# 64 of 512 plain columns move to the other column groups in a graph layer's edge sum

## The reference

```python
s_j = silu(x_j[:, 384:] @ W1 + b1) @ W3 + b3        # x_j = x[src]
edge_basis = rbf * cutoff @ W2 + b2                 # 20 sines of the edge weight
s1, s2, s3 = thirds of (s_j * edge_basis)
v_msg = v_j * s1[:, :, None] + s3[:, :, None] * edge_attr1[:, None, :]
x = x + segment_sum(concat([v_msg, s2]), dst)
... second message: node-wise, h from norms, summed over the same edges
x = layernorm(input + x)
```

## Time and profile before

| | |
|---|---|
| time, median of 3 runs | 641.67 us (639.85 to 643.99) |
| profiled execution, span first to last instruction | 638.7 us |
| edge loop with gathers | about 50 to 535 us |
| PE busy, matmul records | 538.3 us (84%), 5281 |
| granted TensorE clock, mean | 0.936 |
| DMA, mean | 197 GB/s |

### The profile page before, as it was taken

How to read it: one execution, slowest core, us unless ns; L and a number is a source line. 1 busy time by engine, 2 the same in 40 slices (tenths; PEclk the granted TensorE clock), 3 DMA queues, 4 the chain that set the end, 5 groups by cost and what they waited for, 6 DMA issues and landing times.

```text
span 638.7 us, 14716 instructions
## 1 busy us (share of the span) xinstructions
PE 538.3 (84%) x5281; PEld 298.4 (47%) x5281; DVE 471.8 (74%) x796; ACT 446.0 (70%) x835; POOL 367.8 (58%) x405
## 2 busy tenths in 40 slices
PE   5647598888988998889978998888998899699996
PEld 3313244444544553555544554554554455355442
DVE  3886577788878877888787887978887768553385
ACT  3333476677877895888797788778797779659300
POOL 8827666666656666666666666766665563532300
PEclk9755797989989999999999999989998899999998
DMA  8837777777777777778777777778777775040122
GB/s 241 302 125 233 223 214 213 225 236 221 215 207 231 218 220 238 218 213 239 214 224 234 226 214 238 209 223 243 215 217 210 226 217 157 18 128 33 36 84 83
DMA packets 48067, 125.83 MB, mean 197 GB/s; under 512 B 9539, under 2 KB 22409, under 8 KB 47985
## 3 DMA queue, kind: packets, MB, share of 16 engines
q0 software_dynamic: 25120, 102.91, 55.0%
q1 hardware_dynamic: 18433, 15.76, 8.0%
q10 hardware_dynamic: 4432, 6.10, 3.0%
HBM read 112.73 MB, written 12.00 MB: 195 GB/s over the span
## 4 chain that ended last, share of the span: by engine, by line
PE 56%; ACT 19%; issue 13%; DVE 4%; another core or an unknown queue 4%; DMA 2%; POOL 1%; SPq 0%; ACTq 0%; DVEq 0%; POOLq 0%
PE psum L1382 11%; PE psum L1487 10%; PE psum L1376 7%; ACT side L708 7%; PE psum L1344 6%; PE psum L1356 6%; ACT scratch L717 6%; PE psum L1337 4%; PE psum L1390 3%; PE psum L1402 2%; PE psum L1366 2%; DMA work<-in_edge_attr 2%; ACT total L722 1%; PE psum L1420 1%
## 5 line engine op out<-in xcount | busy, mean ns | idle before, releaser
L584 POOL DMA_INDIRECT side<-node_table,src_c x234 | 232.6, 994 | 130.5 <-remote 69.5
L708 ACT ACTIVATE side<-key_no,less_key 128x320 bf16<-128x320 f32 x314 | 160.1, 564 | 0.3
L1376 PE MATMUL psum<-side,scratch 128*32 128x512 f32 x468 | 129.7, 631 | 9.0 <-ACT stage L728 7.0
L1382 PE MATMUL psum<-side,scratch 128*32 128x128 f32 x1404 | 126.6, 285 | 10.7 <-issue 10.2
L717 ACT ACTIVATE scratch<-side,one_f 128x640 bf16<-128x640 bf16 x157 | 129.0, 822 | 0.0
L1071 DVE TENSOR_TENSOR side<-side,psum 128x512 f32<-128x512 f32 x117 | 79.9, 683 | 46.2 <-PE psum L1344 23.5
L584 POOL DMA_INDIRECT work<-node_table,src_c x80 | 80.7, 1008 | 57.4 <-remote 26.7
L1074 DVE TENSOR_TENSOR side<-side,psum 128x768 f32<-128x768 f32 x117 | 110.9, 948 | 0.0
L663 ACT CAST scratch<-psum 128x512 bf16<-128x512 f32 x79 | 46.2, 584 | 82.9 <-remote 51.1
L1382 PEld LDWEIGHTS psum<-side,scratch 128*32 128x32 f32 x1404 | 77.9, 112 | 37.1 <-issue 35.0
L1344 PE MATMUL psum<-w2s,scratch 128*128 128x384 bf16 x314 | 81.1, 341 | 2.4 <-issue 2.3
(11 more groups left out here) (226 smaller groups left out, 776.1 us busy)
## 6 DMA issues: line engine op xcount, KB each, us to landing
side<-node_table,src_c POOLq DMA_INDIRECT x234
sum_rows<-stage SPq DMA_DIRECT2D x208, 16.0 KB
sum_rows<-zeros_bf SPq DMA_DIRECT2D x1, 2688.0 KB, 20.7
node_table<-work ACTq DMA_DIRECT2D x8, 320.0 KB, 3.6
scratch<-sum_rows SPq DMA_DIRECT2D x10, 256.0 KB
work<-sum_rows SPq DMA_DIRECT2D x10, 256.0 KB, 2.7
out<-xw SPq DMA_DIRECT2D x9, 256.0 KB
xw<-in_x ACTq DMA_DIRECT2D x1, 1728.0 KB
```

Of the source, the lines that this page charges most:

```text
L584: g.indirect_dma_start(out=rows[i % SLOT_PAIRS][:, j, :], out_offset=None, in_=node_table, in_offset=bass.IndirectOffsetOnAxis(ap=src_c[:, ...
L708: a.activation(key_off[:, b, j, :], key_no[:, :], ACT.Abs, bias=less_key[:, t:t + 1]).then_inc(L["key_off_made"], 1)
L1376: mm(bank[b][j * SPAN:(j + 1) * SPAN, :], hot[:, n % 2, t + j, 0, :], rows[s][:, j, 0:4 * C], start=first, stop=True, skip_group_check=True)
L1382: last = mm(bank[b][(2 + j) * SPAN:(3 + j) * SPAN, k * C:(k + 1) * C], hot[:, n % 2, t + j, 1 + k, :], rows[s][:, j, 4 * C:5 * C], start=f ...
```

## The change

A constant `PLAIN = 448` is new. The plain products of `add_up` cover columns 0 to 448 of the bank in groups 0 and 1. For the last 64 columns there are two new products a pair, one for each tile, with the same one-hot matrices, which write columns 448 to 512 of groups 2 and 3. They stand ahead of the carry and the attribute products. As they start the sum in those groups in the first pair of a group of tiles, the attribute products no longer do. `combine` adds all four groups, so the result is the same sum.

In columns that pass a column group in one pair: groups 0 and 1 had 2 x 512 with two records a product and have 2 x 448, groups 2 and 3 had 2 x 384 and have 2 x 448. Matmul records rise from 5281 by 628, four in each of 157 pairs.

```diff
+PLAIN = 448
...
                 for j in range(2):
-                    mm(bank[b][j * SPAN:(j + 1) * SPAN, :], hot[:, n % 2, t + j, 0, :], rows[s][:, j, 0:4 * C],
+                    mm(bank[b][j * SPAN:(j + 1) * SPAN, 0:PLAIN], hot[:, n % 2, t + j, 0, :], rows[s][:, j, 0:PLAIN],
+                       start=first, stop=True, skip_group_check=True)
+                for j in range(2):
+                    mm(bank[b][(2 + j) * SPAN:(3 + j) * SPAN, PLAIN:4 * C], hot[:, n % 2, t + j, 0, :], rows[s][:, j, PLAIN:4 * C],
                        start=first, stop=True, skip_group_check=True)
                 if i == GP * n + 1:
                     carry(n)
                 for k in range(3):
                     for j in range(2):
                         last = mm(bank[b][(2 + j) * SPAN:(3 + j) * SPAN, k * C:(k + 1) * C], hot[:, n % 2, t + j, 1 + k, :],
-                                  rows[s][:, j, 4 * C:5 * C], start=first and k == 0, stop=True, skip_group_check=True)
+                                  rows[s][:, j, 4 * C:5 * C], start=False, stop=True, skip_group_check=True)
                 last.then_inc(L["summed"], 1)
```

## The result

The changed kernel takes 643.71 us in the median (641.37 to 645.70, 20 runs) beside 641.08 for the kernel before (20 runs). The ratio is 1.0041, 95% interval [1.0026, 1.0056]: slower by 2.6 us, a small loss that is clear of noise. The profiled execution spans 640.3 us.

A forecast was written before the change was run, and what follows sets the result against it. The prediction took the pace of POOL's gathers, not PE, as the bound. Terms of -0.8, +1.4 and +0.8 us gave +1.4 on the 638.7 us span, 640.1; with 3.0 up to the median, 643 us, range 634 to 668.

The forecast's parts named there:

- a hidden change: Main case: in the loop the change falls into time PE would have waited; 641 to 646 us, likeliest 643, chance 55%.
- the term that made the loss: In the steady loop, four more matmul records a pair, 0.18 to 0.38 us, taken as nothing behind PE's slack.
- The term after the last gather: Near 535 us, some seven pairs remain with array time no longer hidden, each saving 0.115 us: -0.8 us.
- pairs without a wait: About 15 pairs whose gathers run on at once; added records cost 0.19 us in half of them: +1.4 us.
- the start: Early stretch of gathers without a gap; four records left over at half clock: +0.8 us, bounds 0 and 3.6.
- the 2.77 us: From the end of a pair's attribute records to the next gather that waited; extra PE work inside it costs nothing.
- the cover: In the steady loop, the 2.77 us before the next waiting gather, said to hide changes in PE's work.
- Passed on only when the gather in progress is over: In the loop, other engines learn of a pair's end on PE about two microseconds late, after POOL's current gather.
- a loop through POOL: Pair ends release POOL's next two gathers, and PE runs little ahead; period 2.2 us of gathers plus about 0.9.
- Feed-bound: Rival, 8%: PE's instruction feed limits the whole loop at 94 ns a matmul; 28 to 59 us more, 670 to 700.
- Slower in places: Rival, 27%: where gathers run back to back each added record waits its turn, 1.17 us a place; 648 to 661.
- Faster by array time: Rival, 10%: PE's array is on the path, so balance pays 10 us, up to 18; 624 to 635, likeliest 632.

The follow-up runs named there:

- the narrow kernel: Changed kernel without the two new products, so the last 64 columns are summed nowhere; ratio 1.0005 to the kernel before, 641.14 us.
- the split one: Changed kernel with the new products of 64 columns kept in column groups 0 and 1; ratio 1.0031 to the kernel before, 642.85 us.
- the slower run with one gather: Kernel before with the slot's halves gathered in turn from the ninth pair on, the first of two such runs; 549.68 us, ratio 0.8556.
- The pause: Kernel before with a one-column write by POOL, and the wait for it, between a pair's two gathers; 570.56 and 571.43 us, ratios 1.0278 and 1.0276.
- the first experiments: The comparison of the first four experimental kernels with the kernel before on one chip, where the kernel before took 640.85 us.
- a rarer wait on POOL: Kernel before with POOL waiting for free slots only at every second pair, for two slots at once; 557.79 us, ratio 1.0008.

## Why the prediction was right

**The forecast.** 643 was said for a hidden change, and 643.71 was measured; as a difference, +1.4 was said and +2.6 came. That the two lie so close is partly luck: none of the three small terms that make up the +1.4 was confirmed at its size, and the term that made the loss stood at nothing. Its main claim, that balance on PE's array is worth nothing because the loop goes by another pace, is shown three ways: the pace of 3.14 us unchanged, nothing gained by array time alone, and the pace gone with one gather a pair.

**Array time.** The saving was put at 0.115 us a pair from the spacing of two records; add_up shows 0.08. The term after the last gather, -0.8 us, can't be told in runs that spread over 4 us; the narrow kernel, which has it and none of the cost, is at +0.3 us with an interval from -1.4 to +2.0. The traces don't show it either: from the start of the last gather to the end of the last pair's sum it is 14.6 us in the kernel before, 14.5 in the narrow one and 14.6 in the changed one.

**Instructions.** They were put at nothing in the loop, 1.4 us in pairs without a wait and 0.8 at the start. The start measured 0.4 by the clock and 1.3 counted from the first gather, in one execution each. The pairs without a wait weren't the mechanism: from 150 to 530 us in the changed kernel there are about 8 of them (129 "issue" gaps less 121) where there had been 15, and none in the kernel with eight more products, which loses 20 us. They are paid back besides, all but a little: the three steps around such a pair, from the pair ahead of it to the second behind, take 9.52 us in the mean in the changed kernel and 9.47 in the kernel before, where three ordinary steps take 9.44. The step that was wrong in size is "Work on PE inside it costs nothing until it outgrows the 2.77 us": the eight additional products cost 0.13 us a pair, also in pairs that ended well inside the cover. The small costs sit in POOL's wait before a pair. Its mean over pairs 32 to 149 is 0.85 us in the kernel before and 0.86 in the narrow one, 0.87 in the changed one, 0.89 in the split one and 1.03 with eight more. In one execution each, 0.02 us in 157 pairs is about the 2.6 us. By what way a later end of PE lengthens this wait I can't say.

**The mechanism.** "Passed on only when the gather in progress is over" describes the executions at 641 us: the update of `summed` comes 0.4 to 0.7 us behind the end of the second gather, whether the pair's sum ended 0.3 or over 2 us before it. The changed kernel at 557 has the same gathers, of 947 ns, and no late update, so gathers alone don't do it. What differs between the two isn't in any view of the profile that I read. The wider claim, that the 3.14 us are a loop through POOL, stands on the run with one gather, on the updates and on the releases in the earlier trace rows. The last part of it, that PE may run only some way ahead of ends that are not yet passed on, is seen at the start of the slower run with one gather (no third sum from 62.9 to 73.1 us) but was not tested. The pause, which would have tested the loop where it matters, never ran in such a comparison.

**The rivals.** Feed-bound: out, by 84 ns a matmul in the changed kernel and by 2.53 us a pair with one gather. Slower in places: out as a mechanism, as the pairs without a wait are fewer and nearly paid back. Faster by array time: out at 641 us and, more surprising, at 557 and with one gather, where I had written 543 to 550 for the changed kernel beside 549.7, and expected 1% of gain at 557. At 557 us the gathers back to back are the bound. With one gather the likely bound is VectorE and ScalarE, 98% busy in the loop. I had taken those two for followers, since over the whole span they are busy only 84% and 80%.

**The Trainium skill.** The 62 ns a matmul of "TensorE: Matmul & The Clock Gate", section "Back-to-back issue gap", with its 39 us, isn't seen: the changed kernel runs the 36 matmul records of a pair with carry in 1.34 us, 37 ns each, and the whole change cost 2.6 us. "Key Properties" of "TensorEngine Tiling (Array Packing)" agrees with the trace as far as PE goes: add_up is 0.08 us shorter with more records in it. Of the kernel's time it says nothing.

**Left open.** Why the kernel takes 641 us in two comparisons and 556 in three. The three were made on three chips other than that of the first experiments, but also later, and of these four comparisons no two share a chip, so chip and time can't be told apart. The chip of the result isn't on record. Open too is whether a pause or a rarer wait on POOL is worth anything at 641. No version with the reference's sums beat the kernel before.

## What to carry to other kernels

Before shortening an engine's work, look at the spacing of the slowest repeating event, here the gathers, and compare it with the engine's own undisturbed step. PE had 84% busy time and 56% of the chain, and nothing was to be had from a shorter add_up. Take the part with the saving alone and the part with the cost alone as two kernels: here the two together told within 0.3% that there was nothing to cancel. And time a change on more than one chip and at more than one time, beside the kernel before each time, since what bounds a kernel may differ between comparisons by more than any change to it.

## What the runs showed of the hardware

- One program had two speeds: the changed kernel spans 640.3 us in one comparison and 553.5 in another, at mean granted clocks of 0.948 both. The kernel before: 641.08, 640.85 and 555.44, 557.15, 556.79 us in five comparisons. The changed kernel's difference lies in the edge loop, which takes 493.0 and 407.5 us from the first pair's end to the last one's; what follows takes 90.2 and 89.6. POOL's waits put down to "remote" go with it, 102.5 us against none.
- With two gathers a pair, and only in the comparisons at 641 us, a pair's semaphore update stands some 2.5 us behind the end of its sum; it is 0.31 us with one gather in the same comparison, and 0.13 with two gathers at 557. Behind a row of gathers without a wait it was 9.7 us late (62.9 to 72.6). With one gather a pair the loop runs at 2.53 us in both (112 gathers of the second run lie 2.53 us apart as well).
- A record of 64 columns lasts 231 ns where one of 448 lasts 556 and one of 128 lasts 276. Records in different column groups overlap, so that 36 of them passed in 1.34 us.
